# Step-by-step gathers, shorter staging leads and PSUM operands in a graph network kernel

## The reference, cut to what matters

```python
# 1: three graph convolutions, widths 32 -> 128 -> 128 -> 32
msg = (h @ W)[src] * norm[:, None];  h = relu(segment_sum(msg, dst) + b)
# 2: attention over edges, 4 heads of 8
scores = einsum('ehd,ehd->eh', q[dst], k[src]) / sqrt(8)
e = exp(scores - segment_max(scores, dst)[dst])
out = x + (segment_sum(e[..., None] * v[src], dst) / segment_sum(e, dst)) @ Wo
# 3: relational layer, 86 edge types, 16 bases
a = tanh(relu(sum((h[src] @ A1 + b1) * (h[dst] @ A2 + b2 + rel_emb[etype])) / sqrt(32)))
nei = segment_sum(a * einsum('eb,ebo->eo', w_comp[etype], einsum('ei,bio->ebo', h[src], weight)), dst)
# 4: tensor product with 9 harmonic parts of each edge (1 + 3 + 5)
base = einsum('ijk,ei,emj->emk', CG, sh[l], feats[src]);  out = segment_sum(base @ W, dst)
```

## Time and profile before

| | us |
|---|---|
| median of 3 runs | 18891.85 |
| lowest and highest | 18883.74, 18925.59 |
| the profiled execution, time | 18947.52 |
| the profiled execution, span | 18945.8 |
| POOL busy | 10120.5 |
| PE busy | 8522.1 |
| DVE busy | 6436.8 |
| ACT busy | 3262.9 |

### The profile page before, as it was taken

One profiled execution on the slowest core, in us unless ns is written; L12 is line 12 of the kernel. 1 busy time (PEld: TensorE's weight loads), 2 busy tenths in 40 slices (PEclk: granted clock), 3 DMA queues, 4 the chain that ended last, 5 costly groups with the idle time before them and its releaser, 6 DMA issues. The chain is left out here.

```text
span 18945.8 us, 216786 instructions
## 1 busy us (share of the span) xinstructions
PE 8522.1 (45%) x45357; PEld 5689.7 (30%) x45358; DVE 6436.8 (34%) x15234; ACT 3262.9 (17%) x5175; POOL 10120.5 (53%) x10318
## 2 busy tenths in 40 slices
PE   4122223444441222234444445577777776344445
PEld 1111112222221111134343323344444445232324
DVE  6222222222222333311111277455555541222222
ACT  1122123444441111110000000111111111000001
POOL 0566665555646666656666433344444441666773
PEclk9555556666665555555555555788888885666666
DMA  2111112222221111121111122111000112111111
GB/s 77 28 25 25 25 25 54 59 60 58 62 53 19 20 19 19 19 80 41 42 42 43 37 55 60 26 23 23 22 23 23 23 22 61 21 20 18 20 19 44
DMA packets 673630, 679.94 MB, mean 36 GB/s; under 512 B 337206, under 2 KB 510625, under 8 KB 670498
## 3 DMA queue, kind: packets, MB, share of 16 engines
q0 software_dynamic: 340624, 383.65, 10.2%
q1 hardware_dynamic: 217122, 250.20, 4.3%
q10 hardware_dynamic: 115056, 38.34, 0.8%
HBM read 510.75 MB, written 157.94 MB: 35 GB/s over the span
## 5 line engine op out<-in xcount | busy, mean ns | idle before, releaser
L703 POOL DMA_INDIRECT rel_ring<-scratch_tab,rel_staged x1664 | 1624.8, 976 | 2057.4 <-DVE rel_staged L692 1585.1
L703 POOL DMA_INDIRECT sh_ring<-scratch_tab,sh_staged x1664 | 1813.8, 1090 | 1107.2 <-DVE sh_staged L692 601.0
L1158 POOL DMA_INDIRECT sum1g_ring<-scratch_parts,sum1g_staged x1568 | 1547.8, 987 | 1168.5 <-SPq L1182 668.4
L1158 POOL DMA_INDIRECT sum0g_ring<-scratch_parts,sum0g_staged x1568 | 1539.6, 982 | 1178.1 <-issue 830.5
L1799 POOL DMA_INDIRECT score_ring<-scratch_tab,score_staged x1664 | 1623.6, 976 | 970.1 <-issue 518.6
L1158 POOL DMA_INDIRECT sum2g_ring<-scratch_parts,sum2g_staged x1568 | 1510.5, 963 | 935.5 <-issue 462.9
L642 PE MATMUL sh_accumulator<-sh_message,sh_onehot 128*128 128x248 f32 x3328 | 1190.9, 515 | 1493.2 <-issue 1093.0
L642 PE MATMUL rel_accumulator<-rel_message,rel_onehot 128*128 128x512 f32 x3328 | 1827.8, 696 | 52.9 <-issue 48.8
L1839 PE MATMUL score_q_edge<-k_q,score_onehot_t 128*128 x3328 | 758.4, 402 | 1370.2 <-ACT score_onehot_t L1788 913.9
L642 PEld LDWEIGHTS sh_accumulator<-sh_message,sh_onehot 128*128 128x128 f32 x3328 | 787.5, 257 | 1896.1 <-issue 1804.2
L1839 PEld LDWEIGHTS score_q_edge<-k_q,score_onehot_t 128*128 128x128 f32 x3328 | 727.8, 330 | 1456.2 <-issue 1456.0
(11 more groups left out here) (422 smaller groups left out, 15341.5 us busy)
## 6 DMA issues: line engine op xcount, KB each, us to landing
scratch_kv<-score_ring SPq DMA_DIRECT2D x208, 256.0 KB
value_ring<-scratch_kv SPq DMA_DIRECT2D x208, 256.0 KB, 2.7
rel_ring<-scratch_tab,rel_staged POOLq DMA_INDIRECT x1672
score_ring<-scratch_tab,score_staged POOLq DMA_INDIRECT x1664
sh_ring<-scratch_tab,sh_staged POOLq DMA_INDIRECT x1664
scratch_totals<-rel_taken SPq DMA_DIRECT2D x102, 256.0 KB
sum0g_ring<-scratch_parts,sum0g_staged POOLq DMA_INDIRECT x1568
sum1g_ring<-scratch_parts,sum1g_staged POOLq DMA_INDIRECT x1568
```

The source lines that it names most:

```text
L703: nc.gpsimd.indirect_dma_start(out=ring[:, q, g, :], out_offset=None, in_=table, in_offset=bass.IndirectOffsetOnAxis(ap=staged[:, q, g:g + ...
L1158: nc.gpsimd.indirect_dma_start(out=ring[:, q % slots, g, :], out_offset=None, in_=table, in_offset=bass.IndirectOffsetOnAxis(ap=staged[:, ...
```

## The change

1. `numbers_in_psum` copies the row of numbers to a PSUM bank, once ahead of the convolutions and once ahead of attention. `_one_hot` (score, value, relational, harmonic), the relational `kind` and `_pair_one_hot` read it from there, in fp32. The convolution one-hot thereby changes its layout to `[P, GT, P]`, and its first input from bfloat16 in SBUF to fp32 in PSUM.
2. The relational `coef` is written to and read from PSUM. In the harmonic stage ACT copies each group's 128 x 72 harmonic parts into PSUM (`factors`, semaphore `spread`), two groups ahead, and DVE's message products read them there.
3. In the convolutions POOL itself loads `W_DONE` and waits for `copied`; `released` is gone. Before every fourth gather (`TURN`) POOL waits for `answered` and increments `asked`; SP waits for `asked` and increments `answered`, one turn ahead. SP answers the turns of a group and only then waits for the group to land, so that turns 1 to 3 of group n + 1 come after group n has landed.
4. In the score stage POOL waits, before group n, until SP has seen group n - 2 landed (`passed`).
5. Relational and harmonic staging runs two groups ahead instead of three.

```diff
 def _one_hot(nc, k, out, first, n=G):
-    return nc.vector.tensor_tensor(out[:], k["iota"][:].unsqueeze(1).to_broadcast([P, n, P]),
+    return nc.vector.tensor_tensor(out[:], k["numbers"][:, 0:P].unsqueeze(1).to_broadcast([P, n, P]),
...
+def numbers_in_psum(nc, ctx, k, name):
+    k["numbers"] = ctx.enter_context(nc.psum_tensor(f"{name}_numbers", [P, BANK], F32))
+    on_vector(nc, name, [lambda: nc.vector.tensor_copy(k["numbers"][:, 0:P], k["iota"][:])])
...
-    return nc.vector.tensor_tensor(out[:], k["columns"][:],
-                                   k["group_rel"][:, n * GT:(n + 1) * GT].unsqueeze(1).to_broadcast([P, P, GT]), ALU.is_equal)
+    return nc.vector.tensor_tensor(out[:], k["numbers"][:, 0:P].unsqueeze(1).to_broadcast([P, GT, P]),
+                                   k["group_rel"][:, n * GT:(n + 1) * GT].unsqueeze(2).to_broadcast([P, GT, P]), ALU.is_equal)
...
@@ _gather_groups @@
-            pool.wait_ge(released, i * SPAN + q + 1)
+            done = nc.s_assert_within(pool.value_load(k["group_words"][0:1, W_DONE, bass.ds(i * SPAN + q, 1)]), 1, NS + BASE,
+                                      skip_runtime_bounds_check_because="a number of pairs")
+            pool.wait_ge(copied, done)
             pool.sem_inc(entered, 1)
             for g in range(GT):
+                if g % TURN == 0:
+                    pool.wait_ge(answered, (i * SPAN + q) * (GT // TURN) + g // TURN + 1)
+                    pool.sem_inc(asked, 1)
...
@@ _pass_groups @@
-    sp.sem_inc(released, slots)
+    sp.sem_inc(answered, 1)
...
+            for c in range(GT // TURN):
+                sp.wait_ge(asked, (i * SPAN + q) * (GT // TURN) + c + 1)
+                sp.sem_inc(answered, 1)
             sp.wait_ge(gathered[q % HALF], (i * 2 + q // HALF + 1) * GT * DMA)
             sp.sem_inc(landed, 1)
...
-            done = sp.value_load(k["group_words"][0:1, W_DONE, bass.ds(i * SPAN + q, 1)], min_val=BASE + 1, max_val=NS + BASE)
-            sp.wait_ge(copied, done)
-            sp.sem_inc(released, 1)
...
@@ score @@
+                        pool.sem_inc(released, 1)
+                        pool.wait_ge(passed, i * R + q + 1)
...
+                sp.sem_inc(passed, 2)
...
                         sp.wait_ge(gathered[q], (i + 1) * G * DMA)
+                        sp.sem_inc(passed, 1)
...
@@ relational @@
-        coef = [sb(f"coef{m}", [P, H, N_BASES]) for m in range(2)]
+        coef = k["numbers"][:, P:P + 2 * H * N_BASES].rearrange("p (m g b) -> p m g b", m=2, g=H)
...
-                                _stage(nc, k, staged, i * R + q + R - 1, (q + R - 1) % R).then_inc(indexed, 1)
+                                _stage(nc, k, staged, i * R + q + 2, (q + 2) % R).then_inc(indexed, 1)
...
@@ tensor_product, scalar @@
-                        act.wait_ge(messaged, i * R + q + R)
-                        act.sem_inc(checked, 1)
+                        act.wait_ge(messaged, i * R + q + 1 + R)
+                        act.wait_ge(loaded[(q + 2) % R], (i + 1 + (q + 2) // R) * DMA)
+                        spread_parts(act, q + 2)
                         load_parts(act, i * R + q + R - 1, (q + R - 1) % R)
...
@@ tensor_product, vector @@
-                        dve.wait_ge(loaded[q], (i + 1) * DMA)
+                        dve.wait_ge(spread, i * R + q + 1)
...
-                        _stage(nc, k, staged, i * R + q + R - 1, (q + R - 1) % R).then_inc(indexed, 1)
+                        _stage(nc, k, staged, i * R + q + 2, (q + 2) % R).then_inc(indexed, 1)
```

71 lines of the change are left out of this document (42 added, 29 removed).

## The result

The changed kernel takes 19751.22 us (median of 4, 19736.48 to 19768.81), the kernel before 18908.72 us (median of 4): the ratio is 1.0437, with a 95% interval from 1.0413 to 1.0462. It is slower by 842 us, where 320 us less were forecast; the time lies outside the range.

What follows compares the result with a forecast made beforehand. POOL's chain of gathers and its pauses were taken to bound most stages, PE relational, DVE value. The terms -241 - 52 - 76 - 30 + 80 = -319 us gave 18,628 us as profiled, 18,573 for the median; range 17,800 to 19,270.

Steps and rivals of the forecast that it cites:

- What bounds the kernel: By stage: POOL's gather chain and pauses in convolutions, score and harmonic; PE in relational; DVE in value.
- holds: PE's results are held back while gathers run; work resumes some microseconds after POOL runs dry; cause not in the profile.
- PSUM operands: Long gathers all become 945 ns: harmonic -241 us, score -52, convolutions -76 (half of 152).
- rival C: Convolutions 1 and 3, score, harmonic: handshake and shorter runs thin out holds; half gives 17,823 us, all 17,072; chance 0.22.
- The Trainium skill's rule on two SBUF inputs: DVE instructions with two SBUF inputs contend with GpSimd reading SBUF; with at most one, outside 2-port modes, they do not.
- The convolution one-hot: Convolutions: 1.08 us slower per pair, 637 us more DVE work, lying in idle time, so taken as 0.
- rival B: Convolutions 3 and 1: each pause grows by one pair, 5.1 us; +413 us, hence 18,986; chance 0.12.
- Value: Value stage: its one-hot, 1446 ns, gets up to 218 ns shorter; up to 45 us, taken as 30.
- Handshake and score gate: Convolutions: turns answered in time, cost 0, otherwise 235 us; score's wait for group n - 2 costs 0.
- Shorter leads: Harmonic: POOL runs dry earlier and DVE waits for ACT's copy, +80 us; relational staging 0, up to 50.
- Rival A: Harmonic: a lead of two makes POOL run dry every second group, 104 pauses, +762 us, hence 19,255; chance 0.17.
- Rival D: Gathers: one SBUF input or the SBUF output still holds them, so only costs are left, 18,972 us; chance 0.06.

Runs made afterwards that it cites:

- the PSUM operands alone: Kernel before plus only the change's operands in PSUM, old handshake, gate and leads: 0.9519 on the chip without holds, 1.0467 on one with holds.
- the spare operation: Two kernels: the PSUM operands alone plus an unread DVE one-hot per group, SBUF/PSUM inputs swapped between score and harmonic: 19,964.57 and 19,966.51 us.
- the operands back in SBUF: The PSUM operands alone, same instructions, but these operands in SBUF: 18,784.29 us against 18,969.71 of the kernel before, 0.9899.
- the gaps: The PSUM operands alone, with POOL also waiting for its own transfers to land: 19,250.31 us, 1.0158 of the kernel before.
- the pacing alone: Kernel before plus only handshake, score gate and shorter leads: 1.0009 on the chip without holds, 1.0073 on one with holds.

## Why the prediction was wrong, point by point

- **What bounds the kernel.** Right as a description: POOL's chain and its pauses. Wrong for the relational stage. POOL waits there for 1585 us, but PE's results are held back there too; the stage took 3611 us where the holds are and 2463 and 2479 us where they are not, and it lost 233 us with the change. "Faster gathers buy nothing" was true, and that they could cost something was not considered.
- **PSUM operands, the step that failed.** That all gathers would take 945 ns was right, and so was the way to reckon their worth where there are no holds (378 us for 378 in the harmonic stage). The step "in the harmonic and score stages I take the whole, since POOL's chain and the pauses after it set the end" is the failure: it took the pauses as given while the gathers changed. They were not. In the harmonic stage of the changed kernel the gathers' busy time fell by 244 us, as forecast, and POOL's idle time grew by 423. With the PSUM operands alone that stage got longer by 287 us (2647 to 2934), where 241 were to be gained; the spare operation, the operands back in SBUF and the gaps show that stretches and gaps among the gathers shorten the standstills. The prediction had the evidence for such a tie before it ("the work resumes only when POOL runs dry"). It used it for the gain in rival C, and for a loss only so far that pauses in the convolutions might eat up the gain (bounds 0 and 152), never that they could grow by more.
- **The Trainium skill's rule on two SBUF inputs**, cited from "SBUF — State Buffer", section "Who interferes with whom", agrees with the traces: gathers of 943 to 950 ns in the mean in every stage with the PSUM operands, 2.5 to 3.0 us beside a one-hot of 2.28 us with two. The rule says who waits; it does not say that the wait costs the kernel time.
- **The convolution one-hot and rival B.** 2284 ns against 2300 forecast. Its cost was taken at 0, and rival B priced it at 5.1 us per pause, with pauses of 13 us in convolution 3 as its sign. About half of that came: the 49 pauses over 3 us there last 11.7 us in the mean with the PSUM operands, against 9.0 before, and with the pacing alone they stay at 9.5. Whether the longer one-hot adds to that, beside gathers that run evenly, was not isolated: with its operands in SBUF there are 8 such pauses left, and convolutions 2 and 3 are shorter than before. The score stage, whose operations kept their length, got longer all the same.
- **Value.** 24 or 25 us in each pair of runs, 30 forecast; its one-hot takes 1225 ns.
- **Handshake and score gate.** Forecast 0 with an upper bound of 235 us. With the leads they cost 1.0073 on a chip with holds: +23, +101, +22 in the convolutions, +30 in score. Where there are no holds the pacing costs 1.0009 (0.9999 to 1.0018). The bound held, the value did not. No pause of the changed kernel's convolutions stands within a group of 16, which was to be the sign of the handshake's price. Rival C, that they thin out the holds, is out for the convolutions and the score stage (39, 47, 49 and 81 pauses with the pacing alone, 34, 46, 47 and 81 before on that chip); in the harmonic stage, with the shorter lead alone, pauses did fall, from 34 to 20.
- **Shorter leads.** Forecast +80 us in the harmonic stage; measured -66 us alone and -104 us with the PSUM operands on the same chip. The sign was wrong. Alone, the shorter lead halved the pauses over 3 us (33 to 16); with the PSUM operands their number stayed (100, 101) and each got shorter (8.9 to 7.7 us). That a gap which comes earlier ends a standstill earlier would fit the second case, but neither is shown by a run of its own. In the relational stage it is +58 us alone (0 to 50 forecast).
- **Rival A** described what the timeline of the harmonic stage came to show, a pause every second group (103 pauses, 730 us, against 104 and 1040), but for the wrong reason: with the lead of three it is there as well. **Rival D** is out by the gathers of 943 to 946 ns.
- **Chances and range.** The case that came true, gathers relieved and holds longer for it, was none of the cases. The 0.32 for slower rested on A and D, which did not act, and on B, which is at most a part of the convolutions' share.

The sum of the change on a chip with holds is thus: PSUM operands +894 us (20,099 - 19,206), pacing +148, and together +931.

## What to carry to other kernels

Relieving an engine of a disturbance is a gain only if nothing else lived off it; where a profile shows that work resumes only when a queue runs dry, any edit that makes this queue run more evenly is to be tried by itself before its arithmetic is believed. Wait lists name who came last, not why: POOL's pause "for staging" was put down to DVE, which itself stood still for PE or ACT. With the record of semaphores as thin as it is on these chips (below), a name in such a list wants a second sign. And a ratio measured on one chip may have the other sign on the next, so look at the time of the unchanged kernel first.

## What was not expected of the hardware

- The same kernel took 18,909 us on the first chip, 19,206, 18,970 and 19,171 us on three different ones (of which the first may be one), and 15,923 us on another. On all but the last, work that hangs on PE and ACT stands still while gathers run, and PE's, ACT's and SP's sequencers have hundreds of instructions of about 0.7 us; on the last neither. One edit was worth 0.952 there and 1.047 on one of the others. No chip was gone back to, so the runs do not tell a property of the chip from its state at the time.
- On a chip with standstills an operation of DVE that computes nothing of use shortened a stage by 119 and 134 us against its twin with one input in PSUM, and gaps of 2.3 to 2.5 us in POOL's gathers shortened score from 2710 to 2448 us.
- What a standstill is stays open. The traces show that it comes while gathers run, that most end some 5 us after they stop (in convolution 3 of the changed kernel 5.2 us in the median of 51) though some end before, and that stretched gathers and gaps shorten it. They don't show what lets DVE go late, why only on some chips, or whether a stretch acts through the gather that is late or through the pause that it makes in what the gather issues. The slow sequencer instructions stand where gathers run, and in the harmonic stage a chain of them lies in ACT's part of a pause (17027 to 17032 above); whether they cause the standstills or come from the same source is not shown.
- The traces with standstills also lack most changes of semaphores: they record 77,080 for the kernel before, 73,050 for the changed one and 116,767 for the one with gaps, against 215,927 and 218,880 on the chip without standstills, for about as many instructions. So on those chips a wait is put down to an engine from a third to half of the changes. Whether the recording itself takes part in the standstills is a rival that no run here tests.
